# Moving the heads of queries and keys from tile to tile with DMAs out of SBUF, in place of DMAs through DRAM

## The reference, cut to what matters

```
q, k, v = (l2norm(q), l2norm(k), l2norm(v))
sim = jnp.einsum('bhid,bhjd->bhij', q, k)
attn = jnp.square(jax.nn.relu(sim))
out = jnp.einsum('bhij,bhjd->bhid', attn, v)
out = tanh_norm(out)
```

## Time and profile before

| What | Value |
|---|---|
| Median of three runs | 3130.85 us |
| The profiled execution: its time | 3139.85 us |
| Its span, first to last instruction | 3138.1 us |
| TensorE busy over the span | 2907.1 us, 93% |
| VectorE, ScalarE, GpSimd busy | 67%, 46%, 37% |
| One sample of the first attention | 47.27 us |
| DMA `ks<-kparts`, `qs<-qparts` | 256 + 256 of 128 KB |

### The profile page before, as it was taken

One profiled execution on the slowest core, in us unless ns is written; L12 is line 12 of the kernel. 1 busy time (PEld: TensorE's weight loads), 2 busy tenths in 40 slices (PEclk: granted clock), 3 DMA queues, 4 the chain that ended last, 5 costly groups with the idle time before them and its releaser, 6 DMA issues. The chain is left out here.

```text
span 3138.1 us, 66657 instructions
## 1 busy us (share of the span) xinstructions
PE 2907.1 (93%) x21548; PEld 2217.3 (71%) x21549; DVE 2098.8 (67%) x5372; ACT 1442.7 (46%) x2948; POOL 1157.0 (37%) x966
## 2 busy tenths in 40 slices
PE   3899999999999999999966999999999972999998
PEld 1677777777777777777744666666766652999997
DVE  4577677677677777777734777777777855444444
ACT  0444544545545545445422555555555533444443
POOL 3324434434434334334321233333233324444443
PEclk7899999999999999999987999999999985999999
DMA  3424424424424424324302111111111101554544
GB/s 83 96 70 92 107 66 95 107 62 98 102 62 104 98 66 104 94 70 104 87 22 51 49 47 53 43 42 52 45 54 47 44 33 44 77 76 76 77 77 69
DMA packets 161126, 223.12 MB, mean 71 GB/s; under 512 B 30305, under 2 KB 125730, under 8 KB 161074
## 3 DMA queue, kind: packets, MB, share of 16 engines
q1 hardware_dynamic: 135138, 187.50, 23.9%
q0 software_dynamic: 25936, 34.95, 7.2%
HBM read 125.26 MB, written 97.08 MB: 71 GB/s over the span
## 5 line engine op out<-in xcount | busy, mean ns | idle before, releaser
L66 POOL TENSOR_TENSOR vrn<-vsm,inv_root 128x16 f32<-128x16 f32 x64 | 243.8, 3809 | 285.8 <-DVE vsm L836 285.8
L665 ACT ACTIVATE R<-psA 128x1024 f32<-128x1024 f32 x256 | 262.4, 1025 | 168.4 <-PE psA L1150 164.2
L857 DVE TENSOR_TENSOR PR<-R 128x1024 f32<-128x1024 f32 x256 | 321.3, 1255 | 0.0
L2512 POOL DMA_INDIRECT out_rows<-e_y,e_dest x137 | 213.7, 1560 | 289.8 <-DMA out_rows<-e_y,e_dest 182.2
L1904 DVE TENSOR_REDUCE m_nm<-psC 128x4 f32<-128x1028 f32 (+1 forms) x256 | 239.0, 956 | 72.0 <-PE psC L2177 71.4
L1165 PE MATMUL psA<-PR,V 128*64 128x258 f32 x2048 | 283.4, 398 | 0.0
L670 ACT ACTIVATE oTs<-psA 128x258 f32<-128x258 f32 x256 | 99.1, 387 | 358.1 <-PE psA L1165 352.3
L1783 ACT ACTIVATE m_PT<-psC 128x770 f32<-128x770 f32 x256 | 194.0, 810 | 137.3 <-PE psC L2205 137.3
L1210 PE MATMUL psA<-wout,OT 128*128 128x256 f32 x1024 | 244.6, 382 | 0.4 <-DVE OT L899 0.4
L1698 POOL DMA_INDIRECT xg<-tn,idx x124 | 124.5, 1004 | 318.6 <-DMA xg<-tn,idx 186.6
L1210 PEld LDWEIGHTS psA<-wout,OT 128*128 128x128 f32 x1024 | 188.7, 191 | 24.6 <-DVE OT L899 0.7
(11 more groups left out here) (417 smaller groups left out, 7633.0 us busy)
## 6 DMA issues: line engine op xcount, KB each, us to landing
ks<-kparts SPq DMA_DIRECT2D x256, 128.0 KB, 3.3
qs<-qparts SPq DMA_DIRECT2D x256, 128.0 KB, 3.8
e_x<-xg SPq DMA_DIRECT2D x143, 129.0 KB
xraw<-in_x SPq DMA_DIRECT2D x66, 256.0 KB
qparts<-qh SPq DMA_DIRECT2D x128, 128.0 KB, 2.4
kparts<-kh SPq DMA_DIRECT2D x64, 128.0 KB, 2.5
kparts<-kl SPq DMA_DIRECT2D x64, 128.0 KB, 2.4
qparts<-ql SPq DMA_DIRECT2D x64, 128.0 KB, 2.4
```

The lines of the kernel that those rows point to most:

```text
L66: return pool.tensor_tensor(out, x, e.to_broadcast(list(out.shape)), ALU.pow)
L665: act.activation(R[:, p % 2].rearrange("p a t n -> p t a n"), ps[:, 0:2, :].rearrange("p t (a n) -> p t a n", a=2), ACT.Relu).then_inc(rel ...
L857: dve.tensor_tensor(PR[:, p % 2, :, :, 0:L], R[:, p % 2], R[:, p % 2], ALU.mult).then_inc(prob_done, 1)
L2512: pool.indirect_dma_start(out, bass.IndirectOffsetOnAxis(ap=dest[:, b % XD:b % XD + 1], axis=0), y[:, b % XD], None, compute_op=ALU.add).t ...
```

## The change

The DRAM tensors `kparts` and `qparts` go, with their 10 writes and 16 reads per sample. In their place stand 32 DMAs from SBUF to SBUF per sample, 16 for each half c. Each takes 64 rows of one part (1 KB each) to 16 partitions of `ks` or `qs` (4 KB each). The moves of the high keys wait for `k_sq`, those of the low keys for `kl_done`, of the high queries for `q_sq`, and of the low queries for `ql_done`. The moves for c = 1 read the same tiles, are issued ahead of `load_x`, and wait as before for the pairs of the sample before. Since they read `kh`, ScalarE's `mixer` waits for `moved0` and `moved1` before it writes `eq` there.

```diff
+        MOVES = 16 * 16
-            def keep_parts(tiles, rows, out):
-            def lay_out_keys(c, moved):
-            def lay_out_queries(c, moved):
...
+            def move_heads(to, part, at, moved):
                 for hh in range(2):
+                    sp.dma_start(to(64 * hh + at, hh), part[64 * hh:64 * hh + 64].bitcast(F32)).then_inc(moved, 16)
+
+            def move_keys(part, c, ats, moved):
+                for at in ats:
+                    move_heads(lambda row, hh: ks[row:row + 16, 4 * c:4 * c + 4].bitcast(F32), part[:, c], at, moved)
+
+            def move_queries(part, c, ats, moved):
+                for at in ats:
+                    move_heads(lambda row, hh: qs[row:row + 16, hh, 4 * c:4 * c + 4].bitcast(F32), part[:, c], at, moved)
 
             def spread_heads(j, c):
+                moved = moved1 if c else moved0
+                if c == 0:
+                    sp.wait_ge(k_sq, j + 1)
+                else:
+                    need(sp, sim_done, PAIRS * j)
+                move_keys(kh, c, (0, 32), moved)
                 if c == 0:
                     sp.wait_ge(kl_done, j + 1)
+                move_keys(kl, c, (16, 48), moved)
+                if c == 0:
+                    sp.wait_ge(q_sq, j + 1)
+                move_queries(qh, c, (0, 48), moved)
+                if c == 0:
                     sp.wait_ge(ql_done, j + 1)
+                move_queries(ql, c, (16, 32), moved)
...
                 spread_heads(now, 0)
+                spread_heads(now, 1)
                 sp.wait_ge(x2_ready, i + 3)
                 load_x(at)
-                spread_heads(now, 1)
...
             def mixer(j):
                 act.wait_ge(q_done, j + 1)
+                need(act, moved0, MOVES * j)
+                need(act, moved1, MOVES * j)
```

More of the change, by code:

```diff
@@ L442, in mixer_and_attention @@
             nc, ctx, "sim_done", "relu_done", "prob_done", "av_done", "o_copied", "o_sq", "o_ss", "ss_done", "cleared")
-        kl_done, ql_done, k_out, q_out, moved0, moved1, o_sums, sums_copied, kn_done, other_rows = sems(
-            nc, ctx, "kl_done", "ql_done", "k_out", "q_out", "moved0", "moved1", "o_sums", "sums_copied", "kn_done",
+        kl_done, ql_done, moved0, moved1, o_sums, sums_copied, kn_done, other_rows = sems(
+            nc, ctx, "kl_done", "ql_done", "moved0", "moved1", "o_sums", "sums_copied", "kn_done",
             "other_rows")
@@ L481, in store @@
                 sp.dma_start(a.hs[bass.ds(i, 1)].rearrange("n p m -> p (n m)"), h2[:]).then_inc(h2_stored, 16)
-            def keep_parts(tiles, rows, out):
[L484 to L487, removed]
-            def lay_out_keys(c, moved):
-                for hh in range(2):
[L492 to L495, removed]
@@ L497, in lay_out_queries @@
-            def lay_out_queries(c, moved):
[L499 to L504, removed]
-            def spread_heads(j, c):
+            def move_heads(to, part, at, moved):
+                for hh in range(2):
+                    sp.dma_start(to(64 * hh + at, hh), part[64 * hh:64 * hh + 64].bitcast(F32)).then_inc(moved, 16)
@@ L508, in spread_heads @@
                 if c == 0:
                     sp.wait_ge(kl_done, j + 1)
-                    keep_parts((kh, kl), v.kparts, k_out)
-                    sp.wait_ge(ql_done, j + 1)
[L512 to L520, removed]
+                move_keys(kl, c, (16, 48), moved)
@@ L638, in keys @@
                 act.wait_ge(kT_done, j + 1)
-                need(act, moved1, 128 * j)
+                need(act, moved1, MOVES * j)
                 act.activation(kh[:], ps[:, BKT, :].rearrange("p (c n) -> p c n", c=KT), ACT.Copy)
@@ L1144, in sim @@
                     pe.wait_ge(other_rows, 2)
-                    pe.wait_ge(moved0, 128 * i + 128)
+                    pe.wait_ge(moved0, MOVES * i + MOVES)
                 elif p == 4:
-                    pe.wait_ge(moved1, 128 * i + 128)
+                    pe.wait_ge(moved1, MOVES * i + MOVES)
                 need(pe, relu_done, PAIRS * i + p)
@@ L2738, in build @@
     v.last_fill = (nb + 1) % 2
-    v.kparts = nc.dram_tensor("kparts", (KT, 2, 2, P // 2, L), F32, kind="Internal").ap()
-    v.qparts = nc.dram_tensor("qparts", (KT, 2, 3, P // 2, L), F32, kind="Internal").ap()
     v.xg = nc.dram_tensor("xg", (NEXP * v.rows_e + v.idle_rows, ROW), F32, kind="Internal").ap()
```

## The result

The changed kernel takes 3254.12 us (median of four runs, 3248.15 to 3262.65) against 3130.47 us (median of four): 1.0395 times the time of before, 95% interval 1.0364 to 1.0426. It is 124 us slower. The profiled execution took 3262.65 us with a span of 3261.0. The direction and ScalarE's wait were forecast, at a cost of 76.5 us; the range ended at 3243 us, and TensorE's clock was not in the forecast.

A forecast was written before the change was run, and what follows sets the result against it. TensorE, at work for 93% of the span, was taken as the bound. ScalarE's wait at 2.5 us in each of 30 samples (75 us) and some 1.5 in the first made 76.5, giving 3207 us, range 3126 to 3243.

The forecast's parts named there:

- What bounds the kernel: In a steady sample TensorE is the bound, busy 47.15 of 47.27 us; faster heads can bring at most 6.7 us.
- the removed DMAs are worth nothing: Per sample 10 writes and 16 reads of 128 KB go, off TensorE's path, so a steady sample gains nothing.
- The price of an issue: In SyncE's queue, each of the 32 new moves takes 0.62 us from issue to issue, range 0.47 to 0.66.
- The landing: The last move lands 2.3 us after its issue starts, so ScalarE's mixer can write kh at 866.5.
- The point from which it counts: A start of ScalarE's mixer later than 864.0 lengthens the sample, through VectorE's square and denominators; 2.5 us late.
- Beyond it every us is one more us of the sample.: Past 864.0 mixer's lateness lengthens each sample in full: 2.5 us in each of 30 middle samples, 75 us.
- The first sample: Moves end at 107.6, ekv comes at 109.1 where TensorE used it at 107.89; VectorE's chain some 1.5 us late.
- Rival B: Issues are cheap and the writes pace the moves at 0.54 to 0.60 us: 3 to 60 us more; chance 0.15.
- Rival C: Issues cost 0.47 us as with 32 rows, nothing paces them, no sample grows: 3128 us; chance 0.25.

The follow-up runs named there:

- e7: Changed kernel, but each tile's writer waits only for the moves of its own tile, with VectorE's TensorE wait placed behind ScalarE's: 3132.09 us, 1.0011.
- m1: Small program computing none of the model, SyncE issuing groups of eight SBUF-to-SBUF DMAs of several row shapes: 0.59 to 0.67 us per issue back to back.
- e3: Changed kernel without the four moves of the low queries for c = 1 from the second sample on: 3137.54 us, 1.0023.
- e6: Changed kernel with five products that nobody reads put on TensorE right ahead of mix_keys: 3218.11 us, 1.0290.
- e1: Changed kernel with eq in a tile of its own, the waits for the moves going from ScalarE to VectorE: 3140.26 us, 1.0030.
- e5: e1 with VectorE's two waits for the moves put ahead of those for ScalarE and TensorE, TensorE's last: 3137.97 us, 1.0022.

## Why the prediction was right about the wait and wrong in its size

- **What bounds the kernel, and that the removed DMAs are worth nothing:** right. TensorE's wait for the heads fell by 5.5 us, which is lost in the rest; e7, which has no new wait, is no faster than before.
- **The price of an issue:** 0.62 us from start to start, measured 0.6375 (2.55 for four). Right within its range, though the reason given, 64 source rows, is half of one: m1 shows 0.6 for other rows as well, so the price came out right partly by luck. Over 31 issues the difference is 0.5 us per sample.
- **The landing:** 2.3 us, measured 2.4 to 2.6. With the issues, `mixer` starts 22.28 us after the queue in place of 21.5: 867.25 in the time of the earlier trace rows, where I had 866.5. That is 0.75 us per sample too little.
- **The point from which it counts:** 864.0, measured 864.5 to 864.6 in e3. VectorE's square follows ScalarE sooner than I had added up: in the timelines an instruction often starts before the end shown for the one before. TensorE takes ekv 1.28 us after `mixer` starts, not 1.5. That is 0.5 to 0.6 us too much. With the term above, the wait was to be 2.5 us and is 2.49 in TensorE's timeline: the two errors cancel, which is luck. The path was misread too: the earlier trace rows put VectorE's wait before `denominators` down to TensorE's products (L1037), not to the square, and in the kernel after it is again these products that release it, after 1.35 us.
- **The step that failed: "Beyond it every us is one more us of the sample."** A steady sample with the wait loses 4.0 us for 2.49 us of lateness. The sum had no term for TensorE's clock, so it put at nothing what is slower behind the wait. The clock falls to 0.50 right behind a wait of 2.49 us and stays there for a little over 3 us, in which `mix_keys` takes 3.50 us and not 1.99. Thirty times 1.5 us are 45 us; with them the sum is 76.5 + 45 = 121.5, and 124 were measured. e6, which keeps the wait and fills the idle time, gives 36 of them back. The rows of before showed half speed in the first sample (L1150 took 1.19 us in the earlier trace rows, behind a wait of 3.55, and 0.73 in the earlier trace rows), and I read it as a matter of the start. The trace of before also has a steady sample, of 48.54 us, in which the clock was at 0.50 from 715.2 to 718.6 with TensorE busy throughout; so it can fall without a wait. But in the kernel after it fell behind 29 of the 30 waits of 2.4 us and more, and in e6, which fills this wait, twice between 135 and 1570 us.
- **The first sample:** the heads came sooner, at 98.6 in place of 101.16; `mixer` started at 108.55 and TensorE went on at 109.83, 1.9 us later than before and not 1.5. The second and third samples waited 4.7 and 3.6 us, more than the steady ones; the sum had them as steady. In each of them one of the issues took 1.1 us more, and in the second, which stands ahead of the loop, `load_x` still comes before the moves for c = 1.
- **Rival B**, that the writes pace the moves: false here. In the sample's windows the DMA share is 0.24 to 0.37 while the moves run (1014 to 1034), and the last group landed no later after its issue than the first (2.4 to 2.6 us after 2.6 to 2.7). The rule of the Trainium skill, in "SBUF — State Buffer", section "Door 1: The DMA port swizzle", puts an estimated 0.60 us on such a move. That is just under the 0.6375 between issues, so these runs can't refute it; in m1, 128 KB from 128 partitions to 32 landed one in 0.84 us ((34.8 + 4.4 - 30.3 - 3.0) / 7), slower than the 0.60 that the same rule gives. **Rival C** fell with the price of the issue; e3, in which `mixer` starts 2.6 us earlier, shows that a row of issues which ends early enough costs nothing in a steady sample.

## What to carry to other kernels

Before a tile is made the source of late transfers, list who overwrites it under its other names, and let each writer wait for the transfers of its own tile alone: waiting for all of them turned 32 harmless issues into 124 us. Price a wait on the engine that sets the time not only by its length: look at the granted clock behind it, and add what the following work loses at the lower one. Where no slack is left, work out the threshold from the end of each instruction in a row where the engine doesn't pause, since durations added up overlap (0.5 us in six instructions here).

## What the runs showed of the hardware that I had not expected

- TensorE, busy without a pause before, had its clock at 1.2 GHz for a little over 3 us behind idle times of 2.4 to 2.5 us; after 0.15 us of pause (e6) it stayed at 2.4 GHz. The lower clock came while TensorE still stood idle (0.91 in the window 1035 to 1036) or when it had gone on (1.00 from 1499 to 1500, 0.52 in the next us, TensorE at work from 1499.32). The length of the pause alone didn't decide: after 2.77 us in the last sample of the kernel after, after 1.24 us in one of its middle samples, and after 0.90 and 1.67 us in e6 the eight products took 1.99 us; after 1.51 us in e3 they took 3.42.
- The clock was also at 1.2 GHz for some 3 us at times with TensorE busy throughout, one to nine times between 135 and 1570 us in the traces of before, e1, e5 and e7.
- VectorE started 0.04 us after the end that released it with one wait behind the wait for that end, 0.21 us after it with three behind (e1), and 0.12 with none behind and three ahead (e5).
- SyncE's issue of a DMA took 0.42 to 0.45 us with 32 or 128 rows and DRAM on one side, 0.60 with 64 rows, and 0.59 to 0.67 back to back with SBUF on both sides (32 to 128 KB each).
- Back to back, a move of 64 KB from 64 rows to 16 landed 2.6 us after the start of its issue, from 64 rows to 64 after 2.0 (m1).
